# Cross-attention queries of a batch as one 512-column item, and the order of the first splits in the routed stage

## The chip, the cores and the metric

The kernel runs on one core of one Trainium2 chip. The metric is the device time of one execution in microseconds (us), as the median of three runs. A profile is of one execution, with its own time beside it.

## The reference, cut to what matters

A decoder layer on x of 8 batches, 112 tokens, 512 features: x plus causal self-attention, x plus cross-attention on a context of 375 rows for each batch, x plus a mixture of experts. Each stage sees the layer-normalised x. The cross-attention, with 32 heads of 16:

```
q = x @ Wq.T                     # 112 x 512 for a batch
k, v = interleaved(context @ Wk.T, context @ Wv.T)
q = rmsnorm(q per head);  k = rmsnorm(k per head)
out = softmax(q @ k.T * 16**-0.5) @ v
```

The feed-forward part is a shared expert (704 wide) for every token plus, of eight routed experts (352 wide), the two best for each token.

## The kernel before

Every engine has a program written out by hand (`tensor`, `scalar`, `vector`, `gpsimd`, `sync`), and each engine's queue runs in its order; semaphores tie them together. A product in high precision is three matmuls (`mm3`: high by high, high by low, low by high; L595 to L597), so the weights and activations are split on ScalarE (the high part, `..._hi`, L1144) and on VectorE (the rest, `..._lo`, L1625).

**The cross-attention stage** (about 393 to 690 us of the span) is a loop of 48 steps n. A batch b has six steps (i = n % 6): two halves u = 2b and 2b + 1 of 16 heads each, and three chunks m of 125 context rows. In step n TensorE does, in this order: the scores of chunk n (L852); one thing "aside" (a turned attention output, L879, a turned normalised x, L711, or the gate's product and turn, L838); the key and value rows of chunk n + 4 (`rows_pe`, 12 matmuls of 512 columns into one of the two banks KB, L595 to L597 on wkv); at m = 0 the queries of the next half (`rows_pe(u + 1, "q")`, 12 matmuls of 256 columns on wqx); the turn of the keys of chunk n + 3 (`rows_turn`, L812, two transposes); the values (L869, 16 products, shown as 32 matmuls); and at m = 1 the turn of the queries (`queries_turn`, L819, two transposes, into the free half of their KB bank).

Each item (`items`, keys or queries) goes through a chain: TensorE fills its bank, ScalarE squares it (`rows_square`, L1357), VectorE sums the squares for each head (`rows_sum`, L1880), ScalarE takes the root (`rows_root`, L1150 and L1152), VectorE makes the reciprocal root exact with three small instructions and scales the rows into kn (`rows_finish`, L1888 to L1902), TensorE turns kn, and VectorE copies the result to kT (`k_copy`, L1911) or qT (`q_copy`, L1919). An item may take its bank when the item two before it has been scaled, and, if that was a query item, copied to qT (`kb_wait`).

In VectorE's queue `norm_out(3, b - 1)`, which writes the xn that TensorE turns aside at i = 2, stands behind the k_copy and the rows_sum of step i = 1, and `q_copy` behind it. Ahead of the loop there is a prologue (372 to 393 us), in which the last output tiles of self-attention (`o_pe`) cover the first items; the queries of half 0 are `rows_pe(0, "q")` there.

**The routed stage** is preceded by the shared expert on the first four token tiles, whose sums stand in four banks AC until VectorE adds them to xt (L2307, four instructions of 512 columns). Then come the jobs: three with the shared expert's weights on the other three tiles (`("s", j)`) and then 21 blocks of the routed experts. The weights of job k are read into F[k % 2] and split into E[k % 2] in parts (`part_hi` on ScalarE, `part_low` on VectorE); `splits(n, when)` says which parts are split at which place of job n. For job 0 it gives parts 0 and 3 of job 1, both after the first split of the hidden rows (`up_hi`, `up_low`):

```
return {(0, 2): [(1, 0), (1, 3)], (1, 2): [(2, 0), (2, 3)], ...}.get((k, when), [])
```

On VectorE the order there is: the four adds to xt; `up_mul(1, 0)` (L2033); `up_low(1, 0)`; `part_low(1, 0)`; `part_low(1, 3)`; `up_mul(1, 1)`. TensorE meanwhile runs `up_pe(1, c, a)`, 12 matmuls of 384 columns each: c = 0 and 1 of job 0, then c = 2 of job 1, which needs part 0 of job 1.

Of the kernel before, what the change touches and what calls it, by code (L numbers as in the profile page):

```python
# [86 lines left out]
def decoder_layer(nc, x_d, ctx_d, wqk_d, wv_d, wo_d, wqx_d, wkv_d, gw_d, moe_d, wexp_d, mask_d, cst_d,  # L87
                  out_d):
    stack = ExitStack()
    with stack:  # L90
# [125 lines left out]

        sq = [sbl(f"sq{i}", [MS, 256], F32, "wv") for i in range(2)]
# [13 lines left out]
        qT = [sbl(f"qT{i}", [128, 2, 2, T], F32, "mid") for i in range(2)]  # L231
# [6 lines left out]
        zc = sbl("zc", [T, XH], F32, "wv")  # L238
        gw_f = sbl("gw_f", [128, KC, NE], F32, "wv")
# [101 lines left out]
        keys = [(u, m) for u in range(NU) for m in range(MC)]  # L341
        items = keys[:4] + [(0, "q")]
        for n in range(NK):
            items += keys[n + 4:n + 5] + ([(n // MC + 1, "q")] if n % MC == 0 and n // MC + 1 < NU else [])
# [25 lines left out]
        QT = [KB[at_item[u, "q"] % 2][:, 256:256 + 2 * T] for u in range(NU)]  # L370
# [54 lines left out]
        def splits(n, when):  # L425

            kind, j, k, second = its[n]
            if kind == "s":
                return {(0, 2): [(1, 0), (1, 3)], (1, 2): [(2, 0), (2, 3)], (1, 1): [(3, 0)], (2, 0): [(3, 2)], (2, 2): [(3, 1)], (2, 1): [(4, 2)]}.get((k, when), [])
# [82 lines left out]
        kn_done, tx_full, q_turned = sig("kn_done", items), sig("tx_full", tx_uses), sig("q_turned", range(NU))  # L512
        q_copied, k_copied = sig("q_copied", range(NU)), sig("k_copied", keys)
# [77 lines left out]
        def tensor(e):  # L591
# [174 lines left out]
            def kb_wait(n):  # L766
                if n > 1:
                    w.wait_ge(*kn_done[items[n - 2]])
                    if items[n - 2][1] == "q":
                        w.wait_ge(*q_copied[items[n - 2][0]])  # L770
                else:
                    v = kb_last[n]
                    w.wait_ge(*(pj_act if by_act(v) else pj_dve)[v])

            def rows_pe(u, m):
                n = at_item[u, m]
                b, hf = u // 2, u % 2
                kb_wait(n)
                if m == "q":
                    w.wait_ge(*xT_done[2][b])  # L780
                    w.wait_ge(*wqx_lo[1])
                    for k in range(KC):
                        i = mm3(KB[n % 2][0:T, 0:256], at(xT, ALL, k, toks(b * T, T)), at(wqx, ALL, k, toks(hf * 256, 256)),
                                k == 0, k == KC - 1)
# [30 lines left out]
            def queries_turn(u):  # L815
                n = at_item[u, "q"]
                w.wait_ge(*kn_done[u, "q"])
                for g in range(2):
                    i = e.transpose(QT[u][:, g * T:(g + 1) * T], kn[n % 2][0:T, g * 128:(g + 1) * 128], ident[0:T, 0:T])  # L819
                i.then_inc(*q_turned.did(u))  # L820
# [20 lines left out]
            def score_pe(n):  # L841
                u = n // MC
                w.wait_ge(*k_copied[keys[n]])
                w.wait_ge(*q_copied[u])
                if n:
                    w.wait_ge(*x_exped[n - 1, 3])
                else:
                    for i in range(2, 6):
                        w.wait_ge(*pj_dve[pj_last[i]])
                for g in range(2):  # L850
                    for r in range(4):
                        i = e.matmul(SX[r][0:MS, g * 2 * T:(g + 1) * 2 * T], kT[n % 6][32 * r:32 * r + 32, g, :],  # L852
                                     qT[u % 2][32 * r:32 * r + 32, g, :, :], start=True, stop=True)
                        if g:
                            i.then_inc(*scored_x.did((n, r)))
# [26 lines left out]
            def step(n):  # L882
                u, m = keys[n]
                x = aside(n)
                score_pe(n)
                if x and x[0] == "o":
                    out_pe(x[1])
                elif x and x[0] == "n":
                    norm_turn(*x[1:])
                elif x:  # L890
                    gate_pe(*x[1:])
                if n + 4 < NK:
                    rows_pe(*keys[n + 4])
                else:
                    up_pe(0, (n - NK + 4) // 2, n % 2)
                if m == 0 and u + 1 < NU:
                    rows_pe(u + 1, "q")
                if 0 < n < NK - 3:
                    rows_turn(keys[n + 3])
                value_pe(n)  # L900
                if m == 1 and u + 1 < NU:
                    queries_turn(u + 1)

            def gu_wait(u):
                v = gu_before[u]
                if v[0] == "kn":
                    w.wait_ge(*kn_done[v[1]])
                    if v[1][1] == "q":
                        w.wait_ge(*q_copied[v[1][0]])
# [230 lines left out]
        def scalar(e):  # L1140
# [210 lines left out]
            def rows_square(u, m):  # L1351
# [5 lines left out]
                e.activation(sq[n % 2][0:R, :], KB[n % 2][0:R, 0:256], ACT.Square).then_inc(*squared.did(((u, m), "sq")))  # L1357
# [8 lines left out]
            def rows_root(u, m):  # L1366
                n = at_item[u, m]
                R = T if m == "q" else MS
                w.wait_ge(*summed[u, m])
                w.wait_ge(*consts_set["eps"])  # L1370
                root(0, n, R, ss[n % 2][0:R, :], rr[n % 2][0:R, :], epsc[0:R, 0:1], 1.0 / 16).then_inc(*rooted.did((u, m)))
# [23 lines left out]
            def step(n):  # L1395
# [3 lines left out]
                if m == 1 and u + 1 < NU:  # L1399
                    new += [(u + 1, "q")]  # L1400
# [20 lines left out]
                if m == 0 and u + 1 < NU:  # L1421
                    rows_square(u + 1, "q")
# [5 lines left out]
            def s_hi_act(c, part):  # L1428
# [8 lines left out]
                elif c == 1:  # L1437
                    w.wait_ge(*kb_full[NU - 1, "q"])
# [182 lines left out]
        def vector(e):  # L1621
# [254 lines left out]
            def rows_sum(u, m):  # L1876
# [3 lines left out]
                e.tensor_reduce(ss[n % 2][0:R, :], sq[n % 2][0:R, :].rearrange("p (h d) -> p h d", d=16), X, ALU.add).then_inc(  # L1880
                    *summed.did((u, m)))

            def rows_finish(u, m, between=()):
                n = at_item[u, m]
                R = T if m == "q" else MS
                y, tmp, v = rr[n % 2][0:R, :], rq[n % 2][0:R, :], ss[n % 2][0:R, :]
# [10 lines left out]
                if n > 1:  # L1897
                    v = items[n - 2]
                    w.wait_ge(*(q_turned[v[0]] if v[1] == "q" else tx_full["t", v]))
                if m != "q":  # L1900
                    w.wait_ge(*squared[(u, m), "v"])
                e.tensor_tensor(kn[n % 2][0:R, :].rearrange("p (h d) -> p h d", d=16),  # L1902
                                KB[n % 2][0:R, 0:256].rearrange("p (h d) -> p h d", d=16),
                                y.unsqueeze(2).to_broadcast([R, XH, 16]), ALU.mult).then_inc(*kn_done.did((u, m)))
# [9 lines left out]
            def q_copy(u):  # L1914
                w.wait_ge(*q_turned[u])
                if u > 1:
                    w.wait_ge(*scored_x[MC * (u - 2) + MC - 1, 3])
                w.wait_ge(*half_set[0])
                e.tensor_tensor(qT[u % 2][:, :, :, :],  # L1919
                                QT[u].rearrange("p (g t) -> p g t", g=2).unsqueeze(2).to_broadcast([128, 2, 2, T]),  # L1920
                                half[:, :].unsqueeze(1).unsqueeze(3).to_broadcast([128, 2, 2, T]), ALU.mult).then_inc(
                    *q_copied.did(u))
# [42 lines left out]
            def step(n):  # L1965
# [6 lines left out]
                if m == 1 and u + 1 < NU:  # L1972
                    rows_finish(u + 1, "q")
# [22 lines left out]
                if m == 0 and u + 1 < NU:  # L1996
                    rows_sum(u + 1, "q")
                if m == 1 and u + 1 < NU:
                    q_copy(u + 1)
# [73 lines left out]

            def job_dve(n):
# [229 lines left out]
            for t in range(4):  # L2304
                w.wait_ge(*ac_full[0, NS - 1, t])
                w.wait_ge(*rows_in[t]["tile"])
                e.tensor_tensor(xt[:, t, :], xt[:, t, :], AC[t][:, :], ALU.add).then_inc(*xs_first.did(t))  # L2307

# [405 lines left out]
```

## Time and profile before

| | us |
|---|---|
| median of 3 runs (lowest, highest) | 907.11 (906.88, 907.28) |
| the profiled execution | 907.09 |
| its span | 905.3 |
| TensorE busy in the span | 891.3 |
| VectorE busy | 592.2 |
| ScalarE busy | 466.2 |
| GpSimd busy | 203.9 |

The span runs from the first to the last instruction of the core; the execution's time is 1.8 us longer. Busy times of TensorE come from overlapping matmuls whose ends are modelled, so its real pace is read from the distance between the starts of successive matmuls. The granted TensorE clock is at full speed (1.00) in every stretch of the cross-attention stage and of the routed stage up to the last microseconds.

### The profile page before, as it was taken

Reading aid. Unit: us, or ns where it says so; the run is one execution under the profiler, and the core shown is the slowest. Engines: PE = TensorE matmul, PEld = TensorE weight load, DVE = VectorE, ACT = ScalarE, POOL = GpSimd, SP = SyncE. Lnnn points to the kernel's source line nnn. Section 1 sums busy time; section 2 is a strip of 40 time slices with the busy share of each in tenths; the row PEclk is TensorE's granted clock in tenths of the full one; section 3 lists DMA queues with packets and bytes.
Section 4 is the critical chain, followed back from the end, with each engine's and each line's share of the span. In section 5 each row is a group of like instructions: output and inputs, shape, how many; then the busy total and the mean of one; then the engine's idle time right before and its main releaser. Section 6 shows DMA issues by size and latency. Waiting matters only on the chain.

```text
span 905.3 us, 17930 instructions
## 1 busy us (share of the span) xinstructions
PE 891.3 (98%) x7088; PEld 778.9 (86%) x7088; DVE 592.2 (65%) x1304; ACT 466.2 (51%) x1119; POOL 203.9 (23%) x147
## 2 busy tenths in 40 slices
PE   9999999999999999999999999999999999999995
PEld 8998989898989898877877787778777888999994
DVE  7886575757575635765655655646457878888883
ACT  5543334343434344647666656666575236656651
POOL 0143232323333225201101101011000721132223
PEclk9999999999999999999999999999999999999998
DMA  6221242323212115141201001000053787999973
GB/s 223 65 93 41 88 129 94 123 94 123 94 53 95 40 47 180 35 129 30 64 3 36 25 13 36 13 24 13 1 175 113 262 274 295 365 283 302 295 204 46
DMA packets 42195, 104.56 MB, mean 115 GB/s; under 512 B 8208, under 2 KB 18560, under 8 KB 40192
## 3 DMA queue, kind: packets, MB, share of 16 engines
q1 hardware_dynamic: 37808, 94.23, 30.7%
q0 software_dynamic: 4304, 9.19, 5.0%
q8 instruction: 56, 0.92, 0.4%
q14 instruction: 27, 0.22, 0.1%
HBM read 75.57 MB, written 18.65 MB: 104 GB/s over the span
## 4 chain that ended last, share of the span: by engine, by line
PE 95%; DVE 2%; issue 1%; ACT 1%; POOL 0%; DVEq 0%; POOLq 0%
PE bank L595 24%; PE bank L596 23%; PE bank L597 23%; PE bank L852 5%; PE bank L869 5%; PE bank L695 3%; PE bank L671 3%; PE bank L683 1%; PE bank L711 1%; PE bank L812 1%; PE bank L978 1%; PE bank L879 1%; PE bank L986 1%; PE bank L819 1%; PE bank L724 1%
## 5 line engine op out<-in xcount | busy, mean ns | idle before, releaser
L1377 ACT ACTIVATE ee<-bank 125x448 f32<-125x448 f32 x192 | 91.2, 550 | 28.8 <-PE bank L852 28.8
L1625 DVE TENSOR_TENSOR E_lo<-F,E_hi 128x940 fp32r<-128x940 f32 (+3 forms) x62 | 80.8, 1322 | 2.9 <-ACT E_hi L1144 2.8
L595 PE MATMUL bank<-wkv_hi,ctx_hi 128*125 128x512 f32 x192 | 80.1, 417 | 0.0
L2321 POOL TENSOR_TENSOR ctx_lo<-ctx_f,ctx_hi 128x500 fp32r<-128x500 f32 x24 | 30.6, 1278 | 208.2 <-ACT ctx_hi L1144 208.2
L596 PE MATMUL bank<-wkv_hi,ctx_lo 128*125 128x512 f32 x192 | 76.3, 397 | 0.0
L597 PE MATMUL bank<-wkv_lo,ctx_hi 128*125 128x512 f32 x192 | 75.8, 395 | 0.0
L1144 ACT ACTIVATE E_hi<-F 128x940 fp32r<-128x940 f32 (+3 forms) x62 | 67.7, 1139 | 6.7 <-PE bank L597 3.6
L2321 POOL TENSOR_TENSOR wqk_lo<-wqk_f,wqk_hi 128x1024 fp32r<-128x1024 f32 x14 | 35.1, 2505 | 155.5 <-ACT wqk_hi L1144 155.5
L2431 POOL DMA_INDIRECT out<-yg,meta x21 | 39.1, 1863 | 129.3 <-DVE yg L2063 64.4
L1911 DVE COPY kT<-bank 128x250 f32<-128x250 f32 x48 | 20.1, 418 | 69.0 <-PE bank L812 68.8
L595 PE MATMUL bank<-wv_hi,xT_hi 128*128 128x256 f32 x224 | 63.6, 284 | 0.1
L597 PE MATMUL bank<-wv_lo,xT_hi 128*128 128x256 f32 x224 | 62.7, 280 | 0.0
L596 PE MATMUL bank<-wv_hi,xT_lo 128*128 128x256 f32 x224 | 62.7, 280 | 0.0
L1144 ACT ACTIVATE wshi<-wqk_f 128x1024 fp32r<-128x1024 f32 x12 | 12.7, 1061 | 87.8 <-DVE wqk_f L1682 87.8
L595 PE MATMUL bank<-E_hi,xgT_hi 128*128 128x352 f32 x168 | 56.7, 337 | 0.2 <-DVE E_lo L1625 0.2
L597 PE MATMUL bank<-E_lo,xgT_hi 128*128 128x352 f32 x168 | 54.3, 323 | 0.0
L596 PE MATMUL bank<-E_hi,xgT_lo 128*128 128x352 f32 x168 | 54.2, 322 | 0.0
L1357 ACT ACTIVATE sq<-bank 125x256 f32<-125x256 f32 (+1 forms) x64 | 24.5, 383 | 56.8 <-PE bank L597 56.5
L852 PE MATMUL bank<-qT,kT 32*125 32x224 f32 x768 | 49.8, 373 | 0.0
L1763 DVE TENSOR_TENSOR xa<-xa,bank 128x512 f32<-128x512 f32 x56 | 37.7, 685 | 17.7 <-PE bank L597 17.3
L1223 ACT ACTIVATE pp<-sm,nm 112x112 f32<-112x112 f32 x128 | 47.7, 376 | 0.0
L869 PE MATMUL bank<-ee,vb 125*32 125x112 f32 x1536 | 46.8, 262 | 0.0
(411 smaller groups left out, 2569.8 us busy)
## 6 DMA issues: line engine op xcount, KB each, us to landing
F<-wexp SPq DMA_DIRECT2D x14, 1408.0 KB, 7.9
F<-wexp SPq DMA_DIRECT2D x14, 768.0 KB, 7.7
wqk_f<-wqk SPq DMA_DIRECT2D x16, 512.0 KB, 4.3
ctx_f<-ctx SPq DMA_DIRECT2D x24, 250.0 KB, 2.7
slots<-zt SPq DMA_DIRECT2D x3, 1799.0 KB, 8.5
xg<-slots SPq DMA_DIRECT2D x21, 256.0 KB, 7.7
wv_f<-wv SPq DMA_DIRECT2D x8, 512.0 KB, 5.5
wo_f<-wo SPq DMA_DIRECT2D x8, 512.0 KB, 3.4
```

What stands on the lines that cost most here:

```text
L595: e.matmul(out, a[0], b[0], start=first, stop=False)
L596: e.matmul(out, a[1], b[0], start=False, stop=False)
L597: return e.matmul(out, a[0], b[1], start=False, stop=last)
L852: i = e.matmul(SX[r][0:MS, g * 2 * T:(g + 1) * 2 * T], kT[n % 6][32 * r:32 * r + 32, g, :], qT[u % 2][32 * r:32 * r + 32, g, :, :], start= ...
L869: i = e.matmul(AB[32 * c:32 * c + VW, r * T:(r + 1) * T], vb[n % 6][:, 8 * (c // 2) + 2 * r + c % 2, :], ee[(4 * n + r) % 8][:, c * T:(c + ...
L1144: return e.activation(out, src, ACT.Copy)
L1223: i = e.activation(pp[g][:, c, :], sm[g][:, c, :], ACT.Exp, bias=nm[g][:, c:c + 1], scale=ISQ, accum_out=rs[g][:, c:c + 1])
L1377: e.activation(ee[(4 * n + r) % 8][:, :], SX[r][0:MS, 0:4 * T], ACT.Exp, scale=0.25).then_inc(*x_exped.did((n, r)))
L1625: return e.tensor_tensor(out, src, high.bitcast(F32), ALU.subtract)
L1763: e.tensor_tensor(xa[:, j, :], xa[:, j, :], PJ[u][:, :], ALU.add).then_inc(*pj_dve.did(u))
L2321: return e.tensor_tensor(out, src, high.bitcast(F32), ALU.subtract)
L2431: e.indirect_dma_start(out_d, bass.IndirectOffsetOnAxis(ap=meta[:, unit_of[j], 0:1].bitcast(U32), axis=0), yg[j % 4][:, :], None, compute_ ...
```

## The change

The queries of a batch, both halves, are one item of 512 columns: 12 matmuls for a batch where there were 24. It is computed at i = 3 (`queries_in(n) == 0`) for the next batch and turned at i = 4, with four transposes that now stand ahead of `rows_turn` and of the values, and the result fills 448 columns of the item's own KB bank. The query item has buffers of its own (sq_q, which lies over both sq, kn_q, ss_q, rr_q, rq_q), and ScalarE's square next to a query item waits for the sum before it. `q_copy(b)` makes two instructions, one for each half, into three buffers qT. In the prologue the item of batch 0 has 512 columns too, and steps n = 0 and 1 have no query item any more.

In the routed stage part 0 of job 1 is split at the first place of job 0 (`(0, 0): [(1, 0)]`): on ScalarE right after the first Silu and ahead of `up_hi(1, 0)`; on VectorE after `up_mul(1, 0)`, which now comes first. The four adds to xt (`first_out`) follow behind that split.

```diff
-                return {(0, 2): [(1, 0), (1, 3)], (1, 2): ...
+                return {(0, 0): [(1, 0)], (0, 2): [(1, 3)], (1, 2): ...
...
-                        i = mm3(KB[n % 2][0:T, 0:256], at(xT, ...), at(wqx, ALL, k, toks(hf * 256, 256)), ...
+                        i = mm3(KB[n % 2][0:T, :], at(xT, ...), at(wqx, ALL, k, ALL), ...
...
-            def queries_turn(u):
-                n = at_item[u, "q"]
-                w.wait_ge(*kn_done[u, "q"])
-                for g in range(2):
-                    i = e.transpose(QT[u][:, g * T:(g + 1) * T], kn[n % 2][0:T, g * 128:(g + 1) * 128], ...)
+            def queries_turn(b):
+                w.wait_ge(*kn_done[2 * b, "q"])
+                for g in range(4):
+                    i = e.transpose(QT[b][:, g // 2, g % 2, :], kn_q[:, g * 128:(g + 1) * 128], ...)
...
-                if m == 0 and u + 1 < NU:
+                if queries_in(n) == 0:
                     rows_pe(u + 1, "q")
+                elif queries_in(n) == 1:
+                    queries_turn((u + 1) // 2)
                 if 0 < n < NK - 3:
                     rows_turn(keys[n + 3])
                 value_pe(n)
-                if m == 1 and u + 1 < NU:
-                    queries_turn(u + 1)
...
+                if n and "q" in (m, items[n - 1][1]):
+                    w.wait_ge(*summed[items[n - 1]])
...
-            def q_copy(u):
+            def q_copy(b):
+                w.wait_ge(*q_turned[b])
...
+                for u in (2 * b, 2 * b + 1):
+                    if u > 2:
+                        w.wait_ge(*scored_x[MC * (u - 3) + MC - 1, 3])
+                    i = e.tensor_tensor(qT[u % 3][:, :, :, :], QT[b][:, u % 2, :, :]....
+                i.then_inc(*q_copied.did(b))
...
                 if kind == "s":
+                    if n == 0:
+                        up_mul(1, 2 * j)
                     for i in splits(n, 0):
                         part_low(*i)
-                    up_mul(1, 2 * j)
+                    if n:
+                        up_mul(1, 2 * j)
+                    else:
+                        first_out()
```

## Rows read from the trace of the kernel before

**Rows 1.** The page's part 1: busy us, share of the span, instructions.

```profile
PE 891.3 (98%) x7088; PEld 778.9 (86%) x7088; DVE 592.2 (65%) x1304; ACT 466.2 (51%) x1119; POOL 203.9 (23%) x147
```

**Rows 2.** The page's part 4: the chain that ended last, by engine.

```profile
PE 95%; DVE 2%; issue 1%; ACT 1%; POOL 0%; DVEq 0%; POOLq 0%
```

**Rows 3.** Timeline of PE, step 24: start us, us, what; 12 query matmuls between.

```profile
504.30 0.28 PE L595 MATMUL bank<-wqx,xT_hi 128*112 128x256 f32 x1
...
505.71 0.38 PE L812 MATMUL bank<-ident,kn 125*128 125x125 f32 x2
```

**Rows 4.** Timeline of PE, step 26: the second and the twelfth 512-column matmul.

```profile
514.42 0.40 PE L596 MATMUL bank<-wkv_hi,ctx_lo 128*125 128x512 f32 x1
...
516.74 0.39 PE L597 MATMUL bank<-wkv_lo,ctx_hi 128*125 128x512 f32 x1
```

**Rows 5.** Timeline of PE and DVE, from step 25's turn into step 26.

```profile
511.14 0.38 PE L812 MATMUL bank<-ident,kn 125*128 125x125 f32 x2
...
511.55 0.42 DVE L1911 COPY kT<-bank 128x250 f32<-128x250 f32 x1 [1.50 <-PE bank L812]
...
511.89 0.41 DVE L1880 TENSOR_REDUCE ss<-sq 125x16 f32<-125x256 f32 x1
...
512.35 0.41 PE L819 MATMUL bank<-ident,kn 112*128 112x112 f32 x2
...
512.95 0.55 DVE L1644 TENSOR_SCALAR xn<-xs,mv,rstd 112x512 f32<-112x512 f32 x1
513.41 0.62 DVE L1919 TENSOR_TENSOR qT<-bank,half 128x448 f32<-128x448 f32 x1
513.66 0.60 PE L711 MATMUL bank<-ident,xn 112*128 112x112 f32 x4
```

**Rows 6.** Groups by line and form: count, busy us, mean ns, idle before.

```profile
L1357 ACT ACTIVATE sq<-bank 112x256 f32<-112x256 f32 x16 | 6.1, 383 | 13.2 <-PE bank L597 13.2
L1144 ACT ACTIVATE vt<-bank 128x512 f32<-128x512 f32 x8 | 4.8, 596 | 14.5 <-PE bank L597 14.5
```

**Rows 7.** Groups by line and form of DVE: one 512-column instruction that reads a bank.

```profile
L1763 DVE TENSOR_TENSOR xa<-xa,bank 128x512 f32<-128x512 f32 x56 | 37.7, 685 | 17.7 <-PE bank L597 17.3
```

**Rows 8.** Timeline of the prologue, the first query item.

```profile
388.76 0.38 ACT L1357 ACTIVATE sq<-bank 112x256 f32<-112x256 f32 x1 [2.00 <-PE bank L597]
...
390.84 0.42 DVE L1902 TENSOR_TENSOR kn<-bank,rr 112x256 f32<-112x256 f32 x1
...
391.32 0.41 PE L819 MATMUL bank<-ident,kn 112*128 112x112 f32 x2
```

**Rows 9.** Timeline of ACT and DVE in job 0 of the routed stage.

```profile
719.19 2.48 DVE L2307 TENSOR_TENSOR xt<-xt,bank 128x512 f32<-128x512 f32 x4
...
722.17 0.53 ACT L1144 ACTIVATE hs0hi<-sg 128x384 fp32r<-128x384 f32 x1 [3.55 <-DVE sg L2033]
722.60 2.85 ACT L1144 ACTIVATE E_hi<-F 128x1536 fp32r<-128x1536 f32 x2
...
724.11 3.43 DVE L1625 TENSOR_TENSOR E_lo<-F,E_hi 128x1536 fp32r<-128x1536 f32 x2 [0.83 <-ACT E_hi L1144]
```

**Rows 10.** Timeline of PE there: last matmul of job 0, first of job 1.

```profile
724.11 0.33 PE L597 MATMUL bank<-xT_lo,E_hi 128*128 128x384 f32 x1
725.92 0.44 PE L595 MATMUL bank<-xT_hi,E_hi 128*128 128x384 f32 x1 [1.48 <-DVE E_lo L1625]
```

**Rows 11.** Tile F, issues of 710.5 to 711.6 (job 1's weights): issue and landing.

```profile
L2593 SPq DMA_DIRECT2D F<-moe x2: 328/422/515, 710.6 to 711.0; - x2
...
DMA to landing us min/median/max: 7.9/9.5/11.1
```

**Rows 12.** Tile xg, issues of 738 to 739 (first two blocks' rows).

```profile
L2609 SPq DMA_DIRECT2D xg<-slots x2: 331/378/426, 738.3 to 738.7; - x2
...
DMA to landing us min/median/max: 2.7/2.9/3.2
```

**Rows 13.** Timeline of PE where the first of these is turned.

```profile
742.92 0.60 PE L978 MATMUL bank<-ident,xg 128*128 128x128 f32 x4
```

More of the change, by code:

```diff
@@ L215, in pairl @@
             return sbl(name + "_hi", shape, F32R, where), sbl(name + "_lo", shape, F32R, where)
+        sq_q = over("sq_q", [T, D], F32, room["wv"][0])
         sq = [sbl(f"sq{i}", [MS, 256], F32, "wv") for i in range(2)]
@@ L230, in decoder_layer @@
         ee = [sbl(f"ee{i}", [MS, 4 * T], F32, "mid" if i < 6 else "z") for i in range(8)]
-        qT = [sbl(f"qT{i}", [128, 2, 2, T], F32, "mid") for i in range(2)]
+        qT = [sbl(f"qT{i}", [128, 2, 2, T], F32, "mid") for i in range(3)]
         oo = [sbl(f"oo{i}", [128, 4 * T], F32, w) for i, w in enumerate(("mid", "mask"))]
@@ L238, in decoder_layer @@
         zc = sbl("zc", [T, XH], F32, "wv")
+        kn_q = sbl("kn_q", [T, D], F32, "wv")
+        ss_q, rr_q, rq_q = (sbl(n, [T, 2 * XH], F32, "free") for n in ("ss_q", "rr_q", "rq_q"))
         gw_f = sbl("gw_f", [128, KC, NE], F32, "wv")
@@ L341, in decoder_layer, with queries_in @@
         keys = [(u, m) for u in range(NU) for m in range(MC)]
+        def queries_in(n):
+            return n % 6 - 3 if n % 6 in (3, 4) and n // 6 + 1 < NB else None
         items = keys[:4] + [(0, "q")]
         for n in range(NK):
-            items += keys[n + 4:n + 5] + ([(n // MC + 1, "q")] if n % MC == 0 and n // MC + 1 < NU else [])
+            items += keys[n + 4:n + 5] + ([(n // MC + 1, "q")] if queries_in(n) == 0 else [])
         at_item = {it: n for n, it in enumerate(items)}
@@ L368, in decoder_layer @@
         KB, SX, AB = banks[0:2], banks[2:6], banks[6]
-        QT = [KB[at_item[u, "q"] % 2][:, 256:256 + 2 * T] for u in range(NU)]
+        QT = [KB[at_item[2 * b, "q"] % 2][:, 0:4 * T].rearrange("p (u g t) -> p u g t", u=2, g=2) for b in range(NB)]
         jobs = [("s", j) for j in range(3)] + [(kd, q) for q in range(NP - 1) for kd in "po"] + [("o", NP - 1), ("p", NP - 1)]
@@ L511, in decoder_layer @@
         squared = sig("squared", [(it, p) for it in items for p in ("sq", "v") if it[1] != "q" or p == "sq"])
-        kn_done, tx_full, q_turned = sig("kn_done", items), sig("tx_full", tx_uses), sig("q_turned", range(NU))
-        q_copied, k_copied = sig("q_copied", range(NU)), sig("k_copied", keys)
+        kn_done, tx_full, q_turned = sig("kn_done", items), sig("tx_full", tx_uses), sig("q_turned", range(NB))
+        q_copied, k_copied = sig("q_copied", range(NB)), sig("k_copied", keys)
         KR = [(n, r) for n in range(NK) for r in range(4)]
@@ L769, in kb_wait @@
                     if items[n - 2][1] == "q":
-                        w.wait_ge(*q_copied[items[n - 2][0]])
+                        w.wait_ge(*q_copied[items[n - 2][0] // 2])
                 else:
@@ L843, in score_pe @@
                 w.wait_ge(*k_copied[keys[n]])
-                w.wait_ge(*q_copied[u])
+                w.wait_ge(*q_copied[u // 2])
                 if n:
@@ L852, in score_pe @@
                         i = e.matmul(SX[r][0:MS, g * 2 * T:(g + 1) * 2 * T], kT[n % 6][32 * r:32 * r + 32, g, :],
-                                     qT[u % 2][32 * r:32 * r + 32, g, :, :], start=True, stop=True)
+                                     qT[u % 3][32 * r:32 * r + 32, g, :, :], start=True, stop=True)
                         if g:
@@ L908, in gu_wait @@
                     if v[1][1] == "q":
-                        w.wait_ge(*q_copied[v[1][0]])
+                        w.wait_ge(*q_copied[v[1][0] // 2])
                 elif v[0] == "oo":
@@ L1370, in rows_root @@
                 w.wait_ge(*consts_set["eps"])
-                root(0, n, R, ss[n % 2][0:R, :], rr[n % 2][0:R, :], epsc[0:R, 0:1], 1.0 / 16).then_inc(*rooted.did((u, m)))
+                src, to = (ss_q, rr_q) if m == "q" else (ss[n % 2], rr[n % 2])
+                root(0, n, R, src[0:R, :], to[0:R, :], epsc[0:R, 0:1], 1.0 / 16).then_inc(*rooted.did((u, m)))
             def score_exp(n, r):
@@ L1398, in step @@
                 new = [keys[n + 3]] if 0 < n and n + 3 < NK else []
-                if m == 1 and u + 1 < NU:
+                if queries_in(n) == 1:
                     new += [(u + 1, "q")]
@@ L1420, in step @@
                     rows_square(*keys[n + 4])
-                if m == 0 and u + 1 < NU:
+                if queries_in(n) == 0:
                     rows_square(u + 1, "q")
@@ L1879, in rows_sum @@
                 w.wait_ge(*squared[(u, m), "sq"])
-                e.tensor_reduce(ss[n % 2][0:R, :], sq[n % 2][0:R, :].rearrange("p (h d) -> p h d", d=16), X, ALU.add).then_inc(
+                to, src = (ss_q, sq_q) if m == "q" else (ss[n % 2], sq[n % 2])
+                e.tensor_reduce(to[0:R, :], src[0:R, :].rearrange("p (h d) -> p h d", d=16), X, ALU.add).then_inc(
                     *summed.did((u, m)))
@@ L1885, in rows_finish @@
                 R = T if m == "q" else MS
-                y, tmp, v = rr[n % 2][0:R, :], rq[n % 2][0:R, :], ss[n % 2][0:R, :]
+                y, tmp, v = (t[0:R, :] for t in ((rr_q, rq_q, ss_q) if m == "q" else (rr[n % 2], rq[n % 2], ss[n % 2])))
                 w.wait_ge(*rooted[u, m])
@@ L1971, in step @@
                     rows_finish(*keys[n + 3])
-                if m == 1 and u + 1 < NU:
+                if queries_in(n) == 1:
                     rows_finish(u + 1, "q")
@@ L1995, in step @@
                     norm_out(3, b - 1)
-                if m == 0 and u + 1 < NU:
+                if queries_in(n) == 0:
                     rows_sum(u + 1, "q")
-                if m == 1 and u + 1 < NU:
-                    q_copy(u + 1)
+                if queries_in(n) == 1:
+                    q_copy((u + 1) // 2)
             def s_low(c, part):
@@ L2072, in y_out, with first_out @@
                     e.tensor_tensor(xt[:, 4 + t, :], xt[:, 4 + t, :], YB[u][:, :], ALU.add).then_inc(*y_done.did(u))
+            def first_out():
+                for t in range(4):
+                    w.wait_ge(*ac_full[0, NS - 1, t])
+                    w.wait_ge(*rows_in[t]["tile"])
+                    e.tensor_tensor(xt[:, t, :], xt[:, t, :], AC[t][:, :], ALU.add).then_inc(*xs_first.did(t))
             def job_dve(n):
@@ L2303, in vector @@
             part_low(0, 3)
[L2304 to L2307, printed above, removed]
             for n in range(len(its)):
```

39 lines of the change are left out of this document (19 added, 20 removed).

## The prediction

> **What bounds the kernel.** I read the engines' busy shares first [rows 1], then the chain that ended last [rows 2]: TensorE is busy for 98% of the span and holds 95% of the chain, while VectorE stands at 65% and ScalarE at 51%. So the time is TensorE's own work plus its few waits, and both edits must be priced there: as work taken from its queue, and as waits put in or taken out. The reader should then go to the timeline of TensorE in one cross-attention batch and subtract starts, since the durations shown overlap. Twelve query matmuls of 256 columns take 505.71 - 504.30 = 1.41 us, 0.118 each [rows 3], though each is shown as 0.28 long. Ten steps from one 512-column matmul to another take 516.74 - 514.42 = 2.32 us, 0.232 each [rows 4]. In this stage no matmul group starts later than its neighbours' work allows, except by hundredths. Last I read the routed stage's start, where TensorE does wait [rows 10].
>
> **TensorE's work in the cross-attention loop.** Before, each half costs 1.41 for the matmuls and, for its two transposes between the values and the scores, some 0.34 (512.35 to the scores, taken as half a hundredth either way; four transposes of xn took 0.42 to the next group) [rows 3, 5]. Two halves: 2 x (1.41 + 0.34) = 3.50. After: 12 x 0.232 = 2.79, and four transposes, which now run straight into the two of the keys; between 0.34 for two and 0.42 for four on their own I take 0.38. That is 3.17, so 0.33 less for a batch, and there are 7 such batches (1 to 7): -2.3. The matmuls themselves give almost nothing of it (2.82 against 2.79); it is the second visit for transposes that goes.
>
> By the Trainium skill, "TensorE: Matmul & The Clock Gate", section "Back-to-back issue gap", an isolated gap is N / 2.4 + 2.5 ns, so 109 ns for 256 columns and 216 for 512, a gain of some 2.6 ns a pair and 0.3 us over 96 pairs; the starts in the trace say 4 ns a pair (0.118 twice against 0.232), so the trace agrees. The same section gives a sustained 81 ns at 128 columns and 131 at 512, by which wide matmuls would be much cheaper; that is weighed under the rivals.
>
> **New waits in the loop.** Four places, each counted from T, the start of the key transposes of a step.
>
> (a) Step i = 2. VectorE, after T = 511.14, does k_copy at T + 0.41, rows_sum at T + 0.75, three small instructions and xn, which ends at 513.50 = T + 2.36; then q_copy. TensorE turns xn at 513.66 = T + 2.52 [rows 5]. With the query transposes gone from step i = 1 it gets there 0.34 earlier, at T + 2.18, and xn, with the 0.06 that a semaphore takes (kn ended at 391.26, its turn began at 391.32 [rows 8]), is there at T + 2.42. That is a wait of 0.24. Before, q_copy behind xn ended at 514.03 and held the key matmuls back by about 0.05; that goes. Net +0.19, for 7 batches +1.3.
>
> (b) Step i = 5. Its key matmuls use the bank of the query item and wait for q_copied. q_copy stands behind k_copy and rows_sum, so its first half starts at about T + 1.08; the copies start 0.53 apart and one lasts 0.62 [rows 5]; the second ends at T + 2.23 and is seen at T + 2.29. TensorE comes at T + 2.18. +0.11, for 7 batches +0.8.
>
> (c) Step i = 4 waits for the scaled keys of the step before, and their sum now stands with a wider one: square 112x512 about 0.60 (0.38 for 256, 0.60 for a 128x512 read of a bank [rows 6]), sum and scaling about 0.68 each (0.685 for 512 columns from a bank [rows 7]; 0.41 and 0.42 for 256 [rows 5, 8]). The scaled keys come at about T + 2.5. TensorE comes at T + 2.8 where the gate's product stands ahead of it, which covers it, and at T + 2.2 in batch 0, where there is none: +0.3 once. Without that cover it would be 0.3 in every batch.
>
> (d) The wide item itself has 5.7 us from its last matmul to its turn (the rest of step 3, scores, gate, key matmuls), and its chain takes about 3.7. The waits of ScalarE's squares for the sum before are met long before. Step i = 0 becomes 1.41 shorter for VectorE, whose queue is full there; what it leaves late is k_copy, by my count at 0.45 ahead of the turn that needs its bank. Nothing.
>
> **The prologue.** The item of batch 0 grows by 12 x (0.232 - 0.118) = +1.38, two more transposes +0.19. Its chain ended just in time before: kn at 391.26, turn at 391.32, with the output tiles as cover [rows 8]. Now square, sum and scaling add 0.22 + 0.27 + 0.26 = 0.75, and nothing covers that: +0.79 with the small instructions. q_copy has a second half (+0.53) ahead of the first scores, of which about 0.1 shows. Steps 0 and 1 lose their query item: -(1.5 + 0.34). Sum +0.6.
>
> Cross-attention in all: -2.3 + 1.3 + 0.8 + 0.3 + 0.6 = +0.7. The edit costs a little more than it gives.
>
> A section of the Trainium skill speaks against this edit: "Perfetto Trace Analysis", "Optimizing Scalar/DVE Operations", where ScalarE and VectorE aren't saturated but cause bubbles on other engines, breaking instructions up may let work end sooner. Here they are joined instead. The busy shares [rows 1] show the condition, and by that rule the sum would be on the side of the waits, as it is here.
>
> **The routed stage.** TensorE's last matmul of job 0 starts at 724.11, so the next could start at 724.29 (384 columns, by their starts 0.18 apart); it starts at 725.92, waiting for the low part of part 0 of job 1 [rows 10]. That is 1.63 us. The chain behind it: VectorE does the four adds (719.19, 2.48 long), `up_mul`, then ScalarE `hs0hi`, and only then E_hi at 722.60, E_lo at 724.11 [rows 9]. ScalarE had been idle for 3.55 before 722.17, so since 718.62 [rows 9]. The weights, issued at 710.6, land 7.9 later, at 718.5 [rows 11]. So after the change E_hi(1, 0) runs from 718.65 to 720.1, VectorE, when TensorE's second group is there, does `up_mul` at about 720.0, and E_lo from 720.5 to 722.25. That is 2 us ahead of TensorE at 724.29: the wait goes whole. What is late next: the four adds now end at 724.7 and `up_low` at 725.2, but the banks and the hidden rows are wanted at 730.1 - 1.6 = 728.5; part 3 of job 1 (landing 711.0 + 11.1 = 722.1 [rows 11]) is split by 726.8 and the second hidden rows by 728.5, wanted at 729.1. Then the first block's rows: the xg transfer issued at 738.3 lands 2.7 later, at 741.0 [rows 12], set by the scatters and not by this edit. TensorE turned it at 742.92 [rows 13] and will now load it at about 741.1 to 741.3. Just enough. From there on loads follow use. So -1.6; lower bound of the gain 0, upper 1.63.
>
> **Sum.** 907.1 + 0.7 - 1.6 = 906.2, made against the profiled 907.09 (span 905.3 and 1.8 around it), 0.02 from the median of 907.11. That is 0.1% and below what can be told: about 0.2%, or 1.8 us, either way.
>
> **Rivals.**
>
> A. The waits (a), (b), (c) and in the prologue don't come, since some instruction runs earlier than I counted: -2.3 - 0.3 - 1.6 gives 902.9, with half of them about 904.5. For it: each is only 0.1 to 0.2 long. Against: (a) is read off directly. Chance 0.16.
>
> B. The routed gain is lost again: the wait moves to xg, where the margin is 0.1, or the scatters come later because the weights of job 3 are asked for earlier. Then 907.1 + 0.7 = 907.8. Chance 0.17.
>
> C. Slower. In step i = 4 the scaled keys come late in every batch, since VectorE can't start `rows_finish` before the wide sum. The cover is 0.3; from a chain 0.3 longer than counted each 0.1 costs 0.7 us. If the wide sum and square cost twice a 256-column one (0.82, 0.76) and the root queues behind, the chain is some 0.7 longer, 0.4 shows in 7 batches, and with the prologue's own share the time is 909.5. Chance 0.12.
>
> D. A 512-column matmul really occupies TensorE for little more than a 256-column one: by the durations shown 192 x 0.28 - 96 x 0.39 = 16 us, 890. The starts speak against it. Chance 0.02. The Trainium skill's sustained gaps (the section above; 256 taken between as about 98 ns, an estimate) would give 96 x 65 ns = 6 us; the 0.232 in the trace is not 0.131, so the trace disagrees.
>
> The forecast has 0.50 (its own range 905.0 to 907.3), and 0.03 is for none of these. Range 903.2 to 908.9. Faster than 905.3: A, D and a fifth of the forecast, 0.28; slower than 908.9: C and a rest, 0.14; the same 0.58.
>
> **What the profile of the changed kernel would show.** Query matmuls 0.232 apart; L711 at i = 2 starting at T + 2.42 with VectorE's xn as releaser; key matmuls of i = 5 released by q_copy; the first query turn some 0.8 after the output tiles; no idle before the first matmul of job 1; the first xg turn with little or no wait. I would be wrong if the wide chain misses its turn in step 4, or if xg lands later than 741.

## The result and the profile after

The changed kernel takes 909.54 us (median of 10, 909.28 to 911.36) against 907.15 for the kernel before on the same chips (median of 10, 906.76 to 907.77): a ratio of 1.0028, 95% interval 1.002 to 1.0037. It is slower by 2.4 us, where the forecast was 906.2 with a range up to 908.9. The execution whose profile is shown took 910.98, with a span of 908.9.

The page's part 1 of the changed kernel (busy us, share, instructions; [rows 1] before) and its part 4 ([rows 2]):

```profile
PE 891.6 (98%) x6992; PEld 773.8 (85%) x6992; DVE 586.9 (65%) x1264; ACT 462.2 (51%) x1095; POOL 204.9 (23%) x147
```

```profile
PE 94%; DVE 3%; issue 1%; ACT 1%; POOL 0%; POOLq 0%; DVEq 0%
```

Busy times say nothing here: TensorE has 96 instructions less and the same 891 us. TensorE's waits from 370 us on, by what ended them (us in total, times, longest):

```profile
PE bank L604 <- issue: 2.8, 1, 2.8
PE bank L720 <- DVE xn L1656: 0.7, 4, 0.2
PE bank L827 <- DVE kn_q L1918: 0.7, 1, 0.7
PE bank L604 <- DVE kn L1918: 0.3, 1, 0.3
PE bank L604 <- DVE E_lo L1637: 0.2, 1, 0.2
```

Three of these five lines are in the prediction: (a) is L720, the prologue's wait is L827, and (c) is the 0.3. The wait for E_lo of 1.5 [rows 10] is gone; the 0.2 that is left is another one, at 753.74 in a later job, and the kernel before has it too (0.19 at 750.00). The first line, the longest, is not in the prediction. VectorE's timeline at its place, in the prologue (start us, us, what):

```profile
373.95 0.17 DVE L1908 SCALAR_TENSOR_TENSOR rr<-rq,rr 125x16 f32<-125x16 f32 x1
377.43 0.42 DVE L1918 TENSOR_TENSOR kn<-bank,rr 125x256 f32<-125x256 f32 x1 [3.30 <-PE bank L821]
...
379.42 1.15 DVE L1637 TENSOR_TENSOR zT_lo<-bank,zT_hi 128x448 fp32r<-128x448 f32 x2
```

And TensorE's timeline there: the turn of the first keys, the first matmul of the first output tile, the first of the fourth keys, and the turn behind those.

```profile
376.95 0.38 PE L821 MATMUL bank<-ident,kn 125*128 125x125 f32 x2
380.14 0.77 PE L604 MATMUL bank<-wo_hi,zT_hi 128*128 128x512 f32 x1 [2.81 <-issue]
...
382.83 0.63 PE L604 MATMUL bank<-wkv_hi,ctx_hi 128*125 128x512 f32 x1
...
387.10 0.38 PE L821 MATMUL bank<-ident,kn 125*128 125x125 f32 x2
```

What is to be seen: VectorE stands for 3.30 us ahead of scaling the second keys, until TensorE has turned the first (L821). TensorE turns them only behind the third keys and the last z, at 376.95. Everything behind that scaling in VectorE's queue comes late, zT's low part (zT_lo, from 379.42) among it, which the first output tile needs; TensorE stands 2.81. (In the kernel before, zT_lo starts at 376.92 and the tile at 377.64.) The wait comes from the new line of `rows_finish`, quoted here from the changed kernel:

```python
for v in [v for v in items[max(n - 4, 0):n:2] if v[1] != "q"][-1:]:
    w.wait_ge(*tx_full["t", v])
```

The slice should hold the items that share the buffer kn[n % 2]. For n = 1 it starts at 0, so the second keys wait for the turn of the first, which lie in the other buffer. Before, items 0 and 1 had no such wait. (n = 3 has the wrong item too; `k_copy` of that item already stands ahead of it, so it costs nothing.)

Then the clock. TensorE's windows from 376 on (us, busy us of PE, PEld, DVE, ACT and POOL, granted clock, DMA share, GB/s):

```profile
376.00:380.00 4.00, 1.33 (x12) 1.10 (x11) 2.57 (x6) 1.61 (x5) 0.00 (x0) 0.90 0.00 0
380.00:382.00 2.00, 1.86 (x5) 1.51 (x6) 1.75 (x7) 1.04 (x2) 0.00 (x0) 0.50 0.00 0
382.00:384.00 2.00, 2.00 (x6) 1.60 (x5) 0.89 (x2) 0.00 (x0) 0.00 (x0) 0.50 0.00 0
384.00:386.00 2.00, 2.00 (x6) 1.50 (x6) 0.67 (x2) 0.50 (x2) 0.00 (x0) 0.50 0.40 128
386.00:390.00 4.00, 4.00 (x21) 3.24 (x20) 2.23 (x7) 0.66 (x2) 0.00 (x0) 0.99 0.01 4
```

The granted clock is 0.50 (1.2 of 2.4 GHz) from 380 to 386, and the 0.90 of the window before says that it fell while TensorE still stood. The output tile takes 382.83 - 380.14 = 2.69 us and the twelve key matmuls 387.10 - 382.83 = 4.27, where in the first experiment below, at full clock, they take 379.84 - 378.39 = 1.45 and 382.70 - 379.84 = 2.86: 2.65 us lost.

Of the routed stage two things were forecast. The low part of part 0 of job 1 (VectorE's timeline of the changed kernel) is ready at 728.0, and the adds to xt follow it:

```profile
725.80 0.56 DVE L2049 TENSOR_TENSOR sg<-sg,bank 128x384 f32<-128x384 f32 x1 [1.16 <-PE bank L606]
...
726.27 1.75 DVE L1637 TENSOR_TENSOR E_lo<-F,E_hi 128x1536 fp32r<-128x1536 f32 x1
...
727.94 2.48 DVE L2094 TENSOR_TENSOR xt<-xt,bank 128x512 f32<-128x512 f32 x4
```

TensorE's timeline where job 0 ends, then where the first xg is turned; these answer to [rows 10] and [rows 13]:

```profile
729.60 0.34 PE L606 MATMUL bank<-xT_lo,E_hi 128*128 128x384 f32 x1
729.77 0.34 PE L604 MATMUL bank<-xT_hi,E_hi 128*128 128x384 f32 x1
...
746.67 0.49 PE L986 MATMUL bank<-ident,xg 128*128 128x128 f32 x3
```

From the last matmul of job 0 to the first of job 1 it is 0.17 now and was 1.81. To the xg turn it is 746.67 - 729.60 = 17.07, and was 742.92 - 724.11 = 18.81: 1.74 shorter. So the routed stage gave what it should, and the prologue took more than that back. The first block's rows were forecast to land just in time: here they landed at 746.55, 0.12 ahead of the turn.

### The profile page after: what moved, and what is told of

The parts are those of the page before. It is cut to its first block, busy times and chain, and to the rows that moved or that the text cites. A ratio compares the mean times of both kernels' runs of the same rounds, so it can differ in the third digit from the quotient of the medians.

```text
span 908.9 us, 17687 instructions
## 1 busy us (share of the span) xinstructions
PE 891.6 (98%) x6992; PEld 773.8 (85%) x6992; DVE 586.9 (65%) x1264; ACT 462.2 (51%) x1095; POOL 204.9 (23%) x147
## 4 chain that ended last, share of the span: by engine, by line
PE 94%; DVE 3%; issue 1%; ACT 1%; POOL 0%; POOLq 0%; DVEq 0%
PE bank L604 24%; PE bank L605 24%; PE bank L606 24%; PE bank L860 4%; PE bank L877 4%; PE bank L704 3%; PE bank L680 3%; PE bank L692 1%; PE bank L720 1%; PE bank L821 1%; PE bank L986 1%; PE bank L887 1%; PE bank L994 1%; PE bank L733 1%; DVE xn L1656 0%
## 5 line engine op out<-in xcount | busy, mean ns | idle before, releaser
L604 PE MATMUL bank<-wo_hi,zT_hi 128*128 128x512 f32 x112 | 44.7, 399 | 2.8 <-issue 2.8
```

What stands on the lines that cost most here:

```text
L604: e.matmul(out, a[0], b[0], start=first, stop=False)
```

## The experiments

Each was timed in turns with the kernel before on the same chip. That kernel's median was 906.98 for the first four, 906.88 for the next four, 907.08 for the last three. Differences between two experiments are taken from their differences to it.

**e1_right_parity.** The changed kernel with the slice put right.

```diff
-                    for v in [v for v in items[max(n - 4, 0):n:2] if v[1] != "q"][-1:]:
+                    for v in [v for v in items[max(n - 4, n % 2):n:2] if v[1] != "q"][-1:]:
```

> The changed kernel, in which rows_finish of the second key item no longer waits for the turn of the first (the slice starts at n % 2). Theory W (the loss is that wait, made in the prologue, and the clock it costs): VectorE's idle of 3.3 us at 374 and TensorE's of 2.8 at 377 are gone, the granted clock is 1.00 from 376 to 398, and the time is the forecast one: 911.0 - 2.6 (wait) - 2.7 (clock) = 905.7 against the profiled run, 905.5 to 906.5. Rival L (the loss lies in the wide item and its waits in the loop and in the prologue, so the edit costs 3 to 4 us wherever that wait is): 909 to 909.5, the same as the changed kernel. Rival V (the wait counts, but the lower clock comes anyway from the later prologue): 907 to 908.

Measured: 905.41 (ratio 0.9984, 0.9974 to 0.9994). VectorE scales the second keys without a stop, TensorE goes on, and the clock is full in every window from 372 to 398. VectorE, TensorE and one window of this kernel:

```profile
374.43 0.17 DVE L1908 SCALAR_TENSOR_TENSOR rr<-rq,rr 125x16 f32<-125x16 f32 x1
374.63 0.42 DVE L1918 TENSOR_TENSOR kn<-bank,rr 125x256 f32<-125x256 f32 x1
```

```profile
377.78 0.38 PE L821 MATMUL bank<-ident,kn 125*128 125x125 f32 x2
378.39 0.47 PE L604 MATMUL bank<-wo_hi,zT_hi 128*128 128x512 f32 x1 [0.23 <-issue]
```

```profile
380.00:382.00 2.00, 2.00 (x10) 1.00 0.00 0
```

One bound of one slice turns a loss of 2.4 us into a gain of 1.6. Rival L, the wide item as the cause, is out. Rival V, a lower clock that comes anyway, is out for the median and for the profiled execution; but one of the twelve executions took 910.24 at a mean clock of 0.994 (two of e5's twelve took 910.56 and 911.42 at 0.995), so in single executions the clock can be lower without that wait, and no profile shows where or why.

**e2_wait_alone.** The kernel before with the wait alone.

```diff
                 if n > 1:
                     v = items[n - 2]
                     w.wait_ge(*(q_turned[v[0]] if v[1] == "q" else tx_full["t", v]))
+                elif n == 1:
+                    w.wait_ge(*tx_full["t", items[0]])
```

> The kernel before, with only the one wait put in: rows_finish of the second key item waits for the turn of the first. Nothing else of the change is in it. Theory W: TensorE stands still for some 3 us ahead of the first output tile, then runs at half clock for some 6 us, of which 2 to 3 us are lost: 907.1 + 2.6 + 2.7 = 912.4, and 909.7 if the clock stays up. Rival L: 907 to 907.5, since later work in the prologue has slack that takes the wait up.

Measured: 911.07 (1.0043, 1.003 to 1.0056), 4.1 us slower. TensorE and its windows in this kernel:

```profile
380.30 0.47 PE L595 MATMUL bank<-wo_hi,zT_hi 128*128 128x512 f32 x1 [2.81 <-issue]
```

```profile
380.00:382.00 2.00, 1.70 (x7) 0.92 0.00 0
382.00:384.00 2.00, 2.00 (x7) 0.50 0.03 7
384.00:386.00 2.00, 2.00 (x8) 0.72 0.38 124
```

The same stop and a fall of the clock, but later and for a shorter stretch: the output tile and the twelve key matmuls take 386.09 - 380.30 = 5.79, where they take 381.94 - 377.64 = 4.30 in the kernel before, so the clock cost some 1.5 and not 2.7. The time lies between the two that I had named.

**e4_wait_but_busy.** The changed kernel, its wait as it is, with TensorE occupied meanwhile. The added transposes are no part of the computation.

```diff
             rows_turn(keys[0])
+            pj_wait(("o", last, 0))
+            for _ in range(28):
+                e.transpose(PJ["o", last, 0][:, 0:128], ident[:, :], ident[:, :])
             o_pe(last, (0,))
```

> The changed kernel with its wait as it is, but TensorE doing 28 transposes of a constant tile into the bank of the first output tile while it waits (about 2.7 us of added work that fits the gap; the tile's first matmul starts the bank anew). Theory W with the clock as a consequence of the stop: the first output tile starts no earlier (380.1 to 380.4), the granted clock stays at 1.00, and the time is 911.0 - 2.7 = 908.3 against the profiled run, 908 to 908.6. Rival (the clock falls for another reason, or the half clock costs nothing since other engines set the pace there): 909.5 to 911, as the changed kernel.

Measured: 908.07 (1.001, 1.0001 to 1.0019). TensorE and two windows of it:

```profile
376.84 0.38 PE L821 MATMUL bank<-ident,kn 125*128 125x125 f32 x2
377.06 3.22 PE L1096 MATMUL bank<-ident 128*128 128x128 f32 x28
380.07 0.47 PE L604 MATMUL bank<-wo_hi,zT_hi 128*128 128x512 f32 x1
```

```profile
376.00:380.00 4.00, 4.00 (x38) 1.00 0.00 0
380.00:382.00 2.00, 2.00 (x12) 1.00 0.00 0
```

The tile starts no earlier than in the changed kernel, yet the clock stays at 1.00. Against the kernel before the three stand at +2.39 (as changed), +1.09 (kept busy) and -1.57 (no wait). So the wait itself is 2.66 and the clock 1.30 on the median; in the execution that was profiled the clock was 2.65. The spread of the changed kernel's executions goes with the clock: those at 910.65 to 911.36 list a mean clock of 0.992, the other seven, at 909.28 to 910.05, one of 0.994 to 0.997. Only an execution of the first kind was profiled.

**e3_routed_alone.** The kernel before with the routed stage's new order.

```diff
-                return {(0, 2): [(1, 0), (1, 3)], (1, 2): ...
+                return {(0, 0): [(1, 0)], (0, 2): [(1, 3)], (1, 2): ...
...
                 if kind == "s":
+                    if n == 0:
+                        up_mul(1, 2 * j)
                     for i in splits(n, 0):
                         part_low(*i)
-                    up_mul(1, 2 * j)
+                    if n:
+                        up_mul(1, 2 * j)
+                    else:
+                        first_out()
```

> The kernel before, with only the new order in the routed stage. My term was -1.6, and in the profile of the changed kernel the stretch from the last matmul of cross-attention's end to the first xg turn is 1.74 shorter: 905.4 (905.2 to 905.6). Rival B (the gain is lost again at xg or at the scatters): 906.5 to 907.1.

Measured: 905.19 (0.9981, 0.9972 to 0.9989), 1.79 us less. TensorE at the end of job 0:

```profile
725.16 0.34 PE L597 MATMUL bank<-xT_lo,E_hi 128*128 128x384 f32 x1
725.34 0.34 PE L595 MATMUL bank<-xT_hi,E_hi 128*128 128x384 f32 x1
```

No gap. Rival B of the prediction is out.

**e5_queries_alone.** The other half: the query edit, with the slice put right, and the routed stage as before.

> The kernel before with the wide query item alone, its wait corrected as in the first experiment: the routed stage is in its old order. My terms (-2.3 for TensorE's work, +1.3, +0.8, +0.3 for three waits, +0.6 for the prologue) say 907.1 + 0.7 = 907.8; the difference of the first and the third experiment (905.4 - 905.2) says 907.2. Rival A (the waits don't cost what they show): 903 to 905. Rival C (the keys late in every batch): 909.5 and more.

Measured: 907.74 (1.0015, 1.0006 to 1.0023), 0.86 more than before (0.5 to 2.1); my sum for cross-attention said +0.7. The difference between e1 and e3, +0.22, is smaller, and known to about 1.2 us either way, so the medians don't tell +0.2 from +0.9. The profiles tell more. From the turn of the first keys to the first scores it is 18.75 us in e5 and 16.25 in the kernel before, and from there to the last scores 277.45 and 279.65: +2.50 - 2.20 = +0.3. In e1 the same stretches give +2.47 - 2.15, again +0.3. The rest of e5's median isn't explained by these stretches. In its profile the first keys are turned 0.88 later than in the kernel before; in e3, which has nothing of the query edit, 0.94 later.

**e6_xn_first.** e1, with xn of step i = 2 written one place earlier.

```diff
+                if i == 1 and b:
+                    norm_out(3, b - 1)
                 if m and n + 4 < NK:
                     rows_sum(*keys[n + 4])
-                if i == 1 and b:
-                    norm_out(3, b - 1)
```

> The corrected kernel of the first experiment, with norm_out(3, b - 1) one place earlier in VectorE's queue at i = 1, ahead of rows_sum, whose item is turned only in the next step. If the wait (a) is real and costs what I took for it, the rows of TensorE waiting for xn (4 of up to 0.2, 1.38 in all by the starts) go and the time falls by 1.2 to 1.4: 905.4 - 1.3 = 904.1. Rival: the sum that now stands 0.9 later makes the scaled keys late for step i = 2 or fills VectorE's queue there, and the time stays at 905.4 or rises.

Measured: 905.72 (0.9987, 0.9978 to 0.9996): nothing won, a miss (by the differences to the kernel before, 0.4 more than e1, within the intervals). The first group is GpSimd and VectorE at the end of step 7 in e1, the second the same in e6:

```profile
440.99 1.25 POOL L2343 TENSOR_TENSOR ctx_lo<-ctx_f,ctx_hi 128x500 fp32r<-128x500 f32 x1 [23.86 <-ACT ctx_hi L1152]
441.28 0.42 DVE L1927 COPY kT<-bank 128x250 f32<-128x250 f32 x1 [1.50 <-PE bank L821]
441.62 0.41 DVE L1893 TENSOR_REDUCE ss<-sq 125x16 f32<-125x256 f32 x1
441.94 0.31 DVE L1647 SCALAR_TENSOR_TENSOR rt<-rstd 112x1 f32<-112x1 f32 x1
```

```profile
440.50 1.25 POOL L2343 TENSOR_TENSOR ctx_lo<-ctx_f,ctx_hi 128x500 fp32r<-128x500 f32 x1 [23.85 <-ACT ctx_hi L1152]
440.79 0.42 DVE L1927 COPY kT<-bank 128x250 f32<-128x250 f32 x1 [1.50 <-PE bank L821]
441.13 0.64 DVE L1647 SCALAR_TENSOR_TENSOR rt<-rstd 112x1 f32<-112x1 f32 x1
```

The first small instruction of `norm_out`, one element wide, takes 0.31 in e1 and 0.64 in e6. In both it ends as GpSimd's ctx_lo does: 442.25 beside 442.24, and 441.77 beside 441.75. The kernel before has the same at its place, so the rows from which (a) was read had it in:

```profile
511.26 1.25 POOL L2321 TENSOR_TENSOR ctx_lo<-ctx_f,ctx_hi 128x500 fp32r<-128x500 f32 x1 [24.39 <-ACT ctx_hi L1144]
512.21 0.31 DVE L1635 SCALAR_TENSOR_TENSOR rt<-rstd 112x1 f32<-112x1 f32 x1
```

That suggests that the instruction is held and not at work; e9 to e11 test it. The earlier place has a price as well: e6 has a new wait of 0.2 for a copied kT in the last batch, at 664.12.

**e7_xn_and_q_copy_first.** e6, and q_copy ahead of `rows_sum` at i = 4.

```diff
+                if queries_in(n) == 1:
+                    q_copy((u + 1) // 2)
                 if m and n + 4 < NK:
                     rows_sum(*keys[n + 4])
                 if queries_in(n) == 0:
                     rows_sum(u + 1, "q")
-                if queries_in(n) == 1:
-                    q_copy((u + 1) // 2)
```

> As the one before, and at i = 4 q_copy stands ahead of rows_sum, so the key matmuls of i = 5 find their bank free. If the wait (b) is real: 0.7 to 0.8 less again, 903.4; the idle of 0.1 ahead of the key matmuls of i = 5 goes in seven batches. Rival: nothing more, since q_copy waits for the turn anyway, or the later sum makes the keys of step i = 5 late: 904.1.

Measured: 905.6 (0.9985, 0.9976 to 0.9994). The step (b) shows in TensorE's rows, first of e1 and then of e7; the gate's turn and the key matmuls behind it at i = 5:

```profile
462.92 0.17 PE L846 MATMUL bank<-ident,lT 8*112 8x8 f32 x1
463.13 0.50 PE L604 MATMUL bank<-wkv_hi,ctx_hi 128*125 128x512 f32 x1
```

```profile
462.67 0.17 PE L846 MATMUL bank<-ident,lT 8*112 8x8 f32 x1
462.78 0.50 PE L604 MATMUL bank<-wkv_hi,ctx_hi 128*125 128x512 f32 x1
```

0.21 becomes 0.11, so the wait (b) was real and is gone, in six batches behind the gate's turn and in the first batch behind the scores. The seven are worth 0.6 us in all. The median fell by 0.1, where 0.7 to 0.8 was expected: a miss on the time, though the intervals can't tell 0.1 from 0.6.

**e8_and_prologue.** e7, and in the prologue the fourth keys are turned ahead of the queries; the scores of step 0 wait for the first half of q_copy alone.

```diff
-                w.wait_ge(*q_copied[u // 2])
+                w.wait_ge(*(q_copied[u // 2] if u else half_set[1]))
...
+            rows_turn(keys[3])
             queries_turn(0)
             o_pe(last, (6,))
-            rows_turn(keys[3])
```

> As the one before, and in the prologue the turn of the fourth keys stands ahead of the turn of the queries, so it covers 0.3 of the 0.67 for which TensorE waits for kn_q; the scores of step 0 wait for the first half of q_copy only. Expected 0.4 less: 903.0, with a wait of 0.36 for kn_q and none ahead of the scores. Rival: the scores of step 0 now wait for qT instead, and the time stays at 903.4.

Measured: 904.8 (0.9979, 0.9969 to 0.999), 0.8 less than e7 where 0.4 was expected. The wait for kn_q is 0.45 instead of 0.68 (0.36 was expected). By the starts, from the first of the twelve matmuls ahead of kn_q to the scores it is 398.55 - 393.02 = 5.53 in e8 and 396.35 - 390.50 = 5.85 in e7, so 0.32 less. The rest of the 0.8 is within the intervals. (The profiled execution of e8 took 907.7, its longest; TensorE waits 2.4 us for pp in it, ahead of this stretch.)

**e9_port_free_and_xn_first, e10_port_free_alone, e11_all_together.** ScalarE splits ctx_hi at i = 1 ahead of the third exponential, so GpSimd's ctx_lo is over before VectorE's small instruction comes; put on e6, e1 and e8.

```diff
+                early = ctx_step.get(n, []) if i == 1 else []
+                for k in early:
+                    ctx_hi_act(k)
                 score_exp(n, 2)
                 score_exp(n, 3)
...
-                for k in ctx_step.get(n, []):
+                for k in [] if early else ctx_step.get(n, []):
                     ctx_hi_act(k)
```

> The kernel of e6 (norm_out ahead of rows_sum), and at i = 1 ScalarE splits ctx_hi ahead of the third exponential, so GpSimd's ctx_lo runs 1.3 us earlier. Theory P: in e6 the first instruction of norm_out stood for 0.64 us until ctx_lo on GpSimd ended, so the earlier place won nothing; with ctx_lo gone it takes 0.16, xn ends 0.5 earlier, no turn of xn waits in steps i = 2 of batches 1 to 6, and the 1.35 of waits by the starts falls to 0.1 or so: 905.7 - 1.3 = 904.4. Rival Q (the instruction is long for another reason, such as the copy from a bank ahead of it): it stays 0.64 and the time 905.7.

> The kernel of e1 with the earlier ctx_hi alone. There the instruction takes 0.31, of which 0.15 is the port by theory P: xn comes 0.15 earlier, and the waits of 0.17 to 0.25 fall to 0.05 to 0.1: 905.4 - 0.8 = 904.6. Theory Q: 905.4, the instruction still 0.31.

> The kernel of e8 with the earlier ctx_hi: by theory P 904.8 - 1.3 = 903.5, 0.4% below the kernel before; by Q 904.8.

Measured: e9 904.47 (0.997, 0.9959 to 0.9981), e10 904.71 (0.9973, 0.9963 to 0.9983), e11 903.45 (0.9958, 0.9945 to 0.9972). To the kernels that they were built on: 1.45, 0.80 and 1.55 less, where 1.3, 0.8 and 1.3 were expected. Against e1 alone e9 is 1.0 less, since e6 itself was 0.4 above e1. GpSimd and VectorE in e9, at the same place:

```profile
438.50 1.26 POOL L2346 TENSOR_TENSOR ctx_lo<-ctx_f,ctx_hi 128x500 fp32r<-128x500 f32 x1 [22.57 <-ACT ctx_hi L1152]
...
440.08 0.42 DVE L1930 COPY kT<-bank 128x250 f32<-128x250 f32 x1 [1.50 <-PE bank L821]
...
440.42 0.15 DVE L1650 SCALAR_TENSOR_TENSOR rt<-rstd 112x1 f32<-112x1 f32 x1
```

0.64 has become 0.15, and TensorE has no wait for xn left in the list of waits (e6's for kT is still there). Rival Q is out: the copy from a bank still stands ahead of the instruction. e11, with everything, is 3.6 us under the kernel before and 6.0 under the changed one.

## Why the prediction was wrong

**What failed.** The prologue, forecast at +0.6. The terms in it were about right: the wait for kn_q was to be 0.79; from the first of the twelve output matmuls ahead of it to the turn it is 398.63 - 395.04 = 3.59, of which the matmuls take 12 x 0.231 = 2.77, which leaves 0.82. (The 1.5 that the sum takes off for a query item should have been the 1.41 of [rows 3], so +0.7.) But a wait was missing: the sum puts nothing down for VectorE's new wait. In (d) I looked at ScalarE's new wait alone and found it met long before; the wait that `rows_finish` got for the reader of kn I took to be the old one in other words. I did not put n = 0 to 3 into the slice. The first items are just where `max(n - 4, 0)` changes what it selects, and the item that it hits could be scaled 3.3 us ahead of that turn. It costs 2.66 and, through the clock, for which the prediction has no term either, another 1.3 on the median (e1, e2, e4). 906.2 + 2.7 + 1.3 would have been 910.2, against 909.54; the rest is what (a), (b) and the routed stage came out better than forecast.

**TensorE's work in the loop** (-2.3). Held. The query matmuls of the changed kernel start from 528.44 to 530.98, eleven steps of 0.231, as forecast. That shows their pace alone; the whole term is seen where the waits are gone: the mean of batches 1 to 6, between the starts of their scores, is 36.13 us in the kernel before and 35.73 in e11, 0.40 less, of which 0.05 is q_copy's old hold in step i = 2. That leaves 0.35 for the work, where 0.33 was forecast.

**(a), xn** (+1.3). The size of one wait held, the sum was a little high: step i = 2 takes 5.65 us in e1 and in the changed kernel (mean of batches 1 to 6), 5.48 in the kernel before and 5.43 in e9, so the wait is 0.22 and the net 0.17; with 0.07 in batch 7 that is +1.1 in all. The reason was half wrong. I took the three small instructions ahead of xn to be VectorE's own work behind `rows_sum`; but step i = 2 takes 5.50 in e10, so 0.15 of the 0.22 was GpSimd's, and the cure that follows from my account, e6, cured nothing.

**(b), q_copied** (+0.8). Held: step i = 5 takes 0.09 more in seven batches (5.17 in e1, 5.08 in e7), +0.6. ([rows 5] don't show the 0.53 between the two copies; e1's view of both, 1.15 for two of 0.62, does.)

**(c)** (+0.3 once). Held: the list of waits has 0.3 for kn, once. In the other batches the gate's product covered it, so rival C was wrong.

**Cross-attention in all** (+0.7). Measured apart it is +0.86 (e5), or +0.22 as the difference between e1 and e3; the rows of both e1 and e5 say +0.3. What (a) and (b) cost less accounts for it.

**The routed stage** (-1.6). -1.79 alone (e3), 1.74 in the stretch itself. Rival B's transfer landed 0.12 ahead of the turn in the changed kernel, as the margin of 0.1 had said, but that was luck in part: in the profiles of e3 and e1 it landed 0.6 and 2.2 ahead.

**The forecast of the mechanism without the slip** is e1: 905.41 against 906.2, within the forecast's own range of 905.0 to 907.3.

**The range** reached to 908.9 for a mechanism, rival C, that did not come. It had no room for a new wait in the prologue, because none was looked for there beyond the query item's own.

The Trainium skill, "TensorE: Matmul & The Clock Gate", section "What's actually happening", has TensorE's clock fall to 1.2 GHz when the engine is idle or cold. The traces agree that this follows a stop: 0.50 with the 2.81 us, and 1.00 when transposes fill it (e4).

## What to carry to other kernels

When a rewritten condition is meant to select the same thing as the old one, put its first few indices in by hand: clamped slices and start-up cases are where a wait appears that no steady-state argument sees. Price a stop of TensorE by its length and by the slower clock behind it, and test a suspected clock by filling the gap with work of no use. And when a tiny VectorE instruction shows a length several times its usual one, look at which GpSimd instruction ends at the same moment before reordering anything.

## What the runs showed of the hardware that I had not expected

A stop of 2.81 us in TensorE's queue brought half clock: in the changed kernel's profile before the stop had ended (0.90 on average from 376 to 380) and until 386, in that of e2, with a stop of the same length, only from about 382 (0.92 from 380 to 382) and for half as long. When it fell, and for how long, was not the same in the two executions.

A VectorE instruction with two SBUF inputs of one element for each partition took 0.64 us instead of 0.15, ending 0.02 after a GpSimd instruction that had begun ahead of it (e6). A copy from a bank and a reduction that ran beside the same GpSimd instruction kept their 0.42 and 0.41 (e1). The Trainium skill, "SBUF — State Buffer", section "SBUF: two separate sides", has the rule: VectorE and GpSimd share a pair of ports under an exclusive lock; a VectorE instruction with two SBUF inputs needs it against a GpSimd instruction that reads SBUF, and if the GpSimd one started first it has to stand until that one has ended. These traces agree, with GpSimd's 1.25 us as the holder.
